# A two-layer graph network on 8192 nodes: the table woven in pairs, a new order of the drain, and the verdict behind the second block

## The reference

```python
h = relu(layernorm(x))
wh = (h @ weight).reshape(n, 4, 32)
e = leaky_relu(parent_logit[:, None] + child_logit[None, :], 0.2)
att = softmax(where(adj > 0, e, -9e15), axis=1)        # 4 heads
x = x + einsum('njh,jhf->nhf', att, wh)
h = relu(layernorm(x))
msg = relu((adj @ h) @ W_msg.T + b_msg)
x = x + gru_cell(msg, h)                               # r, z, n gates
```

## Time and profile before

| | us |
|---|---|
| median of 3 runs | 969.53 (964.33 to 972.71) |
| profiled execution | 967.29 |
| its span, first to last instruction | 965.5 |
| granted TensorE clock, mean of the span | 0.838 |

### The profile page before, as it was taken

How to read it: one execution, slowest core, us unless ns; L and a number is a source line. 1 busy time by engine, 2 the same in 40 slices (tenths; PEclk the granted TensorE clock), 3 DMA queues, 4 the chain that set the end, 5 groups by cost and what they waited for, 6 DMA issues and landing times.

```text
span 965.5 us, 12344 instructions
## 1 busy us (share of the span) xinstructions
PE 698.0 (72%) x3381; PEld 439.4 (46%) x3381; DVE 747.9 (77%) x3128; ACT 658.5 (68%) x667; POOL 529.8 (55%) x518
## 2 busy tenths in 40 slices
PE   1577754768776767667777767786776756899997
PEld 0344432445444434445444444454444554466654
DVE  8485777799887977887878788777887874587774
ACT  1676864879697877878787878687787532455542
POOL 4011117574544637272645576575767775777771
PEclk9897977798887887877778788777877767899998
DMA  9999999799999999999999999999993111233232
GB/s 295 420 420 418 421 424 407 282 410 416 412 416 417 414 418 409 398 410 404 406 394 405 399 405 393 405 378 404 401 403 107 37 34 36 59 86 83 73 81 55
DMA packets 55750, 305.51 MB, mean 316 GB/s; under 512 B 13825, under 2 KB 31442, under 8 KB 39296
## 3 DMA queue, kind: packets, MB, share of 16 engines
q1 hardware_dynamic: 27936, 274.74, 69.9%
q0 software_dynamic: 17152, 23.15, 8.3%
q10 hardware_dynamic: 10592, 6.82, 2.4%
HBM read 295.65 MB, written 12.71 MB: 319 GB/s over the span
## 4 chain that ended last, share of the span: by engine, by line
DMA 44%; PE 23%; ACT 12%; DVE 10%; issue 6%; POOL 4%; ACTq 0%; POOLq 0%; DVEq 0%
DMA adj_in<-in_adj 38%; ACT ind L666 11%; PE ps L927 4%; DMA x<-in_x 3%; PE ps L1143 3%; POOL val L557 2%; PE ps L1166 2%; PE ps L1145 2%; PE ps L1167 2%; PE ps L906 1%; DVE cand L1395 1%; PE ps L1168 1%; PE ps L1161 1%; PE ps L1154 1%; PE ps L1158 1%
## 5 line engine op out<-in xcount | busy, mean ns | idle before, releaser
L666 ACT ACTIVATE ind<-adj_in 128x4096 bf16<-128x4096 int32 x128 | 462.2, 3611 | 80.2 <-DMA adj_in<-in_adj 67.0
L927 PE MATMUL ps<-ind,bit_w 128*128 128x512 bf16 x1024 | 291.7, 429 | 46.7 <-ACT ind L666 46.7
L557 POOL DMA_INDIRECT val<-in_adj,val_idx x144 | 154.4, 1072 | 190.0 <-DVE val_idx L1605 139.5
L539 POOL DMA_INDIRECT rows_in<-wh_table,idx x180 | 193.6, 1076 | 62.2 <-issue 62.2
L927 PEld LDWEIGHTS ps<-ind,bit_w 128*128 128x128 bf16 x1024 | 109.5, 109 | 199.3 <-ACT ind L666 62.5
L617 POOL DMA_INDIRECT adj_in<-g_table,idx x96 | 98.2, 1023 | 34.6 <-issue 29.0
L1395 DVE MAX8 cand<-ps 128x8 f32<-128x256 f32 x256 | 91.0, 417 | 24.3 <-PE ps L927 23.9
L972 PE MATMUL ps<-rows_in,ident 128*128 128x132 f32 x120 | 38.8, 424 | 57.1 <-DVE rows_in L1511 57.1
L580 POOL DMA_DIRECT2D wh_table<-rows_in x16 | 12.2, 760 | 107.8 <-DVE rows_in L1349 107.8
L924 PE MATMUL ps<-idx_r,idx_w 128*128 128x512 bf16 x128 | 60.8, 475 | 11.9 <-ACT ind L666 11.9
L972 PEld LDWEIGHTS ps<-rows_in,ident 128*128 128x128 f32 x120 | 30.5, 310 | 64.4 <-DVE rows_in L1511 64.4
(11 more groups left out here) (299 smaller groups left out, 1520.3 us busy)
## 6 DMA issues: line engine op xcount, KB each, us to landing
adj_in<-in_adj SPq DMA_DIRECT2D x128, 2048.0 KB, 17.8
wh_table<-rows_in POOLq DMA_DIRECT2D x16, 264.0 KB, 8.5
g_table<-t_buf ACTq DMA_DIRECT2D x16, 256.0 KB, 25.6
out<-rows_in SPq DMA_DIRECT2D x16, 256.0 KB, 2.4
rows_in<-wh_table,idx POOLq DMA_INDIRECT x180, 6.6
val<-in_adj,val_idx POOLq DMA_INDIRECT x144, 6.3
adj_in<-g_table,idx POOLq DMA_INDIRECT x112, 2.6
ind<-g_table,idx POOLq DMA_INDIRECT x16, 7.1
```

Of the source, the lines that this page charges most:

```text
L539: nc.gpsimd.indirect_dma_start(out=rows_in[:, s % 2, t, k, :], out_offset=None, in_=wh_table, in_offset=bass.IndirectOffsetOnAxis(ap=idx[: ...
L557: nc.gpsimd.indirect_dma_start(out=val2[:, s, k:k + 1], out_offset=None, in_=adj_values, in_offset=bass.IndirectOffsetOnAxis(ap=val_idx2[: ...
L666: nc.scalar.activation(ind[:, (tile * 2 + half) % IND, :], adj_in[:, slot, 0:b - a].bitcast(I32), ACT.Relu, bias=1.0, scale=-1.0, accum_ou ...
L927: ins = nc.tensor.matmul(o, bit_w[:, b, :], ind[:, (tile * 2 + half) % IND, c0:c0 + HALF], start=False, stop=(b == BITS - 1))
```

## The change

Four things are moved; nothing that is computed changes.

1. The table's units stand in pairs at half tiles 2, 4, 6 and 8, so that the last stands at 12 and the row of means at 12 and 13.
2. The verdict goes behind the second block, which now runs unconditionally: DVE's reductions stand behind the mix of group 13, PE's transpose behind the gates of h of group 15, `over_ready` ahead of the last `add_rows`. The load of `over_i` and the branch come at the end of every engine's program. `prepare(q)` waits for the values of its own group.
3. The drain of groups 13 to 15 on PE, DVE and ACT is written in another order (the last group's first): `values(13)` goes from the stream behind the last group's rows; `exps(13)`, `edge_logits(13)` and `differences2(14)` out of the last body; `edges2(14)` to the drain's end, `edges2(15)` behind `prepare(0)`. Some PSUM banks and buffers are others, ACT loads its function tables ahead, and PE's filler matmuls (`keep_busy`, 40 of 512 columns) become 24 of 128.
4. On POOL the ring holds only high sides (11 places), the low sides of groups 8 to 15 have an area of their own. The low sides of groups 8 to 11 are gathered ahead of the wait for `g_table`, those of 12 to 15, values(14) and values(15) between the high sides.

```diff
         def units(m):
-            a = m - 1 + (m > 4) + (m > 8)
-            return (a, a + 1) if m in (4, 8) else (a,) if 1 <= m <= 14 else ()
+            a = m - 1 + (m > 2) + (m > 4) + (m > 6) + (m > 8)
+            return (a, a + 1) if m in (2, 4, 6, 8) else (a,) if 1 <= m <= 12 else ()
...
-                    if m == 14:
+                    if m == 12:
                         mean_row()
...
-                rows_of_last((0, 1))
+                rows_of_last(range(G - 1), (0, 1))
                 pool.wait_ge(idx_done, NG + 1)
-                rows_of_last((2,))
-                values(NG - 2)
-                early_rows(SCAN_PRE + 1)
-                early_rows(SCAN_PRE + 2)
-                values(NG - 1)
-                early_rows(SCAN_PRE + 3)
+                rows_of_last((G - 1,), (0, 1))
+                pool.wait_ge(idx_done, NG + 2)
+                rows_of_last(range(G), (2,))
+                values(NG - 3)
+                for q in range(SCAN_PRE, SCAN_PRE + 4):
+                    low_rows(q)
+                for par in range(2):
+                    pool.wait_ge(g_out[par], 16 * (NG // 2))
+                pool.sem_inc(passed_pool, 1)
+                for q in range(NG):
+                    high_rows(q)
+                    if q == 3:
+                        low_rows(NG - 4)
+                    if q == 5:
+                        low_rows(NG - 3)
+                    if q == 6:
+                        values(NG - 2)
+                    if q == 7:
+                        low_rows(NG - 2)
+                    if q == 8:
+                        values(NG - 1)
+                        low_rows(NG - 1)
...
+                def high_rows(q):
+                    if q >= RING2:
+                        pool.wait_ge(agg2_mm, q - RING2 + 1)
+                    for k in range(SLOTS_OF[0]):
...
-                keep_busy(20)
-                pe.wait_ge(cols2_done, NF)
-                pe.wait_ge(over_done, 1)
-                nc.tensor.transpose(ps[0:1, 3, 0:P], over1[:], ident[:]).then_inc(over_mm, 1)
                 message_columns(NG - 1)
                 message_rows(NG - 1)
...
+                    if q == NG - 2:
+                        pe.wait_ge(cols2_done, NG)
+                        pe.wait_ge(over_done, 1)
+                        nc.tensor.transpose(ps[0:1, 5, 0:P], over1[:], ident[:]).then_inc(over_mm, 1)
...
-                for par in range(2):
-                    dve.wait_ge(values_in[par], 16 * E2 * (NG // 2))
...
+                def prepare(q):
+                    if q >= 2:
+                        dve.wait_ge(agg2_mm, q - 1)
+                    dve.wait_ge(values_in[q % 2], 16 * E2 * (q // 2 + 1))
...
+                prepare(0)
+                edges2(NG - 1)
+                restart()
+                for q in (1, 2):
+                    prepare(q)
+                for q in range(NG):
+                    candidate(q)
+                    if q >= 1:
+                        add_rows(q - 1)
+                    mix(q)
+                    if q + 3 < NG:
+                        prepare(q + 3)
+                    if q + 3 == NG:
+                        edges_sound()
```

More of the change, by code:

```diff
@@ L435, in units, with landed, low_landed, low_rows_of @@
         def units(m):
-            a = m - 1 + (m > 4) + (m > 8)
-            return (a, a + 1) if m in (4, 8) else (a,) if 1 <= m <= 14 else ()
[L439 to L449, removed]
+            a = m - 1 + (m > 2) + (m > 4) + (m > 6) + (m > 8)
+            return (a, a + 1) if m in (2, 4, 6, 8) else (a,) if 1 <= m <= 12 else ()
+        def landed(q):
+            return 16 * SLOTS_OF[0] * (q // RING2 + 1)
+        def low_landed(q):
+            return 16 * SLOTS_OF[1] * (q // SCAN_PRE + 1)
+        def low_rows_of(q):
+            return edges_first[:, q] if q < 4 else edges_more[:, q - 4] if q < SCAN_PRE else edges_low[:, q - SCAN_PRE]
         def rows_of(s):
@@ L543, in rows, with rows_of_last @@
                             ).then_inc(gathered[s % 2], 16)
-                def rows_of_last(slots):
-                    for t in range(G):
+                def rows_of_last(tiles_of, slots):
+                    for t in tiles_of:
                         for k in slots:
@@ new lines, in gates, with rows_back @@
+                def gates(q):
+                    m = msgT[:, q % 2, :]
+                    pe.wait_ge(msg_done, q + 1)
+                    nc.tensor.matmul(ps[:, 0, :], wT[:, 1, :], m, start=False, stop=True).then_inc(gate_mm, 1)
+                    nc.tensor.matmul(ps[:, 2, :], wT[:, 3, :], m, start=True, stop=True).then_inc(gate_mm, 1)
+                    nc.tensor.matmul(ps[:, 1, :], wT[:, 2, :], m, start=False, stop=True).then_inc(gate_mm, 1)
+                def rows_back(q):
+                    pe.wait_ge(new_done, q + 1)
+                    if q >= 1:
+                        pe.wait_ge(fin_done, q)
+                    for t in range(G):
+                        ins = nc.tensor.transpose(ps[:, 4, t * D:(t + 1) * D], newT[:, q % 2, t * D:(t + 1) * D], ident[:])
+                    ins.then_inc(rows_mm, 1)
@@ L1190, in _ @@
[L1190 to L1201 removed]
+                    pe.sem_inc(passed_pool, 1)
@@ L1688, in _ @@
-                row_maximum(NG - 1, (NG - 1) % 2)
-                add_first(NG - 2)
-                edge_logits(NG - 1, (NG - 1) % 2)
-                edges2(NG - 1)
-                finish_norm(NG - 2)
-                weigh(NG - 1, (NG - 1) % 2)
-                V.tensor_reduce(over[:, 5:6], empty[:], AX.X, ALU.max)
-                link(V.tensor_reduce(over[:, 0:5], checks[:], AX.X, ALU.max))
-                for n, bound in enumerate((0.5, float(1 << IBITS), float(NEI0), P + 0.5, 0.5, PIECE + 0.5)):
-                    V.tensor_scalar(over[:, 7 + n:8 + n], over[:, n:n + 1], bound, None, ALU.is_ge)
```

568 lines of the change are left out of this document (283 added, 285 removed).

## The result

The changed kernel takes 69,767.38 us (median of 4 runs, 69,762.8 to 69,781.36) against 967.91 before (median of 4, three of which stood when the prediction was made): 71.87 times as long, 95% interval 71.56 to 72.19. The forecast was 985. The profiled execution took 69,781.36 us.

The account below looks back on a forecast made before the run. The adjacency's DMA stream bounds first, then PE with POOL's gathers hardly ahead; POOL's queue was forecast to bind until group 9. 967.3 + 17.5 + 1.0 - 2.5 = 983.3, plus 2.2 for the median: 985 us, range 973 to 995.

Parts of the forecast that it names:

- its part on the drain: Tail of the stream: last group's index 2.2 us earlier, message table ready at 798.4 to 803.3, taken as 800.
- The index at 758.9: Drain: index of the last group's third rows comes at 758.9, 2.2 us earlier than before.
- POOL's way to the table's wait: Drain: from 758.9 POOL's remaining gathers take 39.5 us, so it stands at the message table's wait at 798.4.
- The table at 800: End of the drain: message table ready between 798.4 and 803.3, taken as 800, when POOL's second block starts.
- Group 9's high rows: Second block: POOL's queue ahead takes 112.8 us, so the last high row of group 9 lands at 914.5.
- 63.2 + 2.5 = 65.7: Second block: 63.2 us from PE's group 9 high side to DVE's last instruction, as before, plus 2.5 for PE's clock.
- The clock's part: PE leaving its wait at group 9 runs at reduced granted clock: 0 to 3.4 us, taken as 2.5.
- The load and branch at the end: Verdict's load and branch now come at the very end, on SP behind the last landing: +1.0 us.
- The weave: Table made two half tiles earlier closes the stream's hole at slice 8: gain 1.5 to 7.6 us, taken as 2.5.
- A: Rival, faster: POOL keeps up in the second block at 0.98 us a gather; 950 on the median; chance 0.07.
- B: Rival, no change: weave brings all the hole cost, clock back at once, table at 798.4; 977 on the median; chance 0.16.
- C: Rival, worse: table at 803.3, clock costs 3.4, early pairs open holes of 4 us; 994 on the median; chance 0.08.

Follow-up runs that it names:

- two-mask kernel: The changed kernel in its own order, with valid2 and late_place given two places each, for even and odd groups: 987.26 us (one run).
- first mend: The changed kernel with edges2(14) put ahead of offsets2(15) on DVE: 993.93 us, 1.023 of before.
- the other order of the same gathers: The two-mask kernel with values(14), values(15) and low rows of groups 12 to 15 put later in POOL's second block: 976.75 us.
- all three edits: The two-mask kernel with values(13) in the stream, low rows of 8 to 13 ahead of the g_table wait, the rest late: 969.48 us, 1.001 of before.
- POOL let go: The two-mask kernel with POOL neither waiting for the verdict nor branching; SP still reads it after its last output: 988.42 us.

## Why the prediction was wrong

**The step that failed** stands in its part on the drain: "The new order puts edges2 of groups 14 and 15 and the checks behind the last group on DVE, which takes time out of that". It was read as time that moves, as was "nothing that is computed changes" in the part on the change. What the runs showed in its place: with `edges2(14)` the reading of two masks moved behind their next writing, the verdict changed, and 68,787 us of general program followed. That the change doesn't do what it says was named among the rivals only for the weave. The diff had it all: `valid3` was given a third place because its readers move behind a writer, `valid2` and `late_place` were not.

**The other terms**, against the two-mask kernel, whose last scan starts at 736.57 (737.80 before):

- The index at 758.9: 758.29. POOL's way to the table's wait, 39.5 us: 759.05 to 799.4, 40.4.
- The table at 800: the first high row starts at 799.87.
- Group 9's high rows, forecast at 914.5: PE goes on at 911.64, after 14.23 us. At group 7 it waited 7.41. The 84 gathers took 108.6 us from the first start to the last, where 111.5 was worked out.
- From there to DVE's last instruction 63.2 + 2.5 = 65.7: 911.64 to 977.83 is 66.2. The clock's part can be read; a window of the two-mask kernel behind the wait, to lay beside the earlier trace rows (us, busy PE, PEld, DVE, ACT, POOL, PEclk, DMA, GB/s):

```profile
911.60:920.00 8.40, 8.36 (x20) 4.62 (x21) 2.60 (x9) 2.99 (x7) 6.27 (x8) 0.68 0.20 49
920.00:940.00 20.00, 20.00 (x94) 12.44 (x92) 15.25 (x33) 11.22 (x21) 15.43 (x16) 1.00 0.31 80
```

By its first line the clock cost 8.4 x (1 - 0.68) = 2.7 us.

- The load and branch at the end, +1.0: mis-sized. The end takes 7.3 us instead of 2.8, +4.5, because POOL's DRAIN comes behind the verdict too.
- The weave, -2.5: mis-sized. The stream ends no earlier; the weave is worth nothing that these runs can tell, and the loss by bytes, 78.0 to 78.4 MB up to 200 us against 78.0 and 78.3 with the old weave in the new drain, is hardly less.

By these, 967.3 + 15.1 + 4.5 = 986.9 for the mended kernel, and 987.26 was measured; the terms are read from that same run, so this takes it apart and doesn't confirm it. That the forecast of 985 lies so near is in part luck: with the weave's 2.5 taken off, as in the sum, the first high row was due at 797.5 and DVE's end at 977.7; the row came 2.4 late, the queue was 2.9 shorter, and 977.83 came out. So without the masks the change would have been 1.5% (two masks) to 2.3% (first mend) slower than before: 15.1 of the 19.6 us as forecast, by POOL's queue and PE's clock behind its wait, and 4.5 by the end. That it is the queue, the other order of the same gathers shows.

The time of the changed kernel was decided by none of the rivals A, B and C; all of them are about the fast program. In that program A and B did not happen. Of C's conditions the early hole is there and cost 7.6 us, where C had 4, but by the late `x`, not by the early pairs.

## What to carry to other kernels

When a step is moved past another, list what it reads and ask who writes that next: here both stood on DVE in program order, nothing waited, and the wrong values were simply read. Where a kernel checks itself and has a slow way out, a mistake shows as time. And when a serial queue is moved, count its entries up to the place where someone waits, not over the whole: the same 114 gathers cost 10 us less in another order.

## What the hardware showed that was not expected

POOL's DRAIN at the program's end took 7.42 us in the two-mask kernel, 8.24 in the kernel before with the verdict moved, and 9.05 with all three edits, while SP's and ACT's took 0.01 and PE's and DVE's 0.07 to 0.08. The Trainium skill (page "VectorE: DVE Perf Modes", section "The DRAIN you can't avoid") tells of a boilerplate DRAIN of about 12 ns on all five engines, from the preamble and postamble. The DRAIN here is recorded under the line where the kernel's own block begins (L487), and whether the page means it too, it doesn't say; SP's and ACT's 13 ns are like it, POOL's is not, and there the measurement decides. POOL's does not wait for gathers in flight: it takes 7.42 us 29 us behind the last gather (two-mask kernel) and 7.42 us again 2.6 us behind it (POOL let go), and likewise 9.05 and 9.05 with all three edits. In the kernel before the record of 928.95 to 953.39 spans the last twelve gathers and ends 8.25 us behind the last of them. What sets its length was not tried; the same 114 gathers in the other order gave 6.93.

The other surprise is that the 1.2 MB more which the first mend had moved by 200 us, 412 GB/s instead of the 384 of the old weave over 120 to 200 us, left the end of the stream where it was; that the slowest DMA engine works on through a hole would explain this, but no run here shows single engines, and it is one pair of runs.
